# Graph network on one core: in the later two aggregations the source features become the stationary operand and the counts of three blocks the moving one

## What is computed

```python
h = relu(layernorm(x))                        # aggregation 0: symmetric norm, elementwise product
out = segment_sum(norm * (h[dst] + (h[dst] * h[src]) @ W1.T + b1), dst)
x = x + leaky(out)
h = relu(layernorm(x))
for Ws, Wn, b in ((Ws0, Wn0, b0), (Ws1, Wn1, b1)):        # aggregations 1 and 2 (GraphSAGE)
    mean = segment_sum(h[src], dst) / max(deg, 1)
    h = h @ Ws.T + mean @ Wn.T + b            # relu between the two
x = x + h
```

## Time and profile before

| | us |
|---|---|
| median of 3 runs | 3779.3 |
| lowest and highest of them | 3773.09, 3781.85 |
| the profiled execution's time | 3776.64 |
| its span, first to last instruction | 3774.9 |
| PE busy in the span | 3351.2 |
| POOL busy | 2654.8 |
| DVE busy | 2582.9 |
| ACT busy | 2222.0 |

### The profile page before, as it was taken

One profiled execution on the slowest core, in us unless ns is written; L12 is line 12 of the kernel. 1 busy time (PEld: TensorE's weight loads), 2 busy tenths in 40 slices (PEclk: granted clock), 3 DMA queues, 4 the chain that ended last, 5 costly groups with the idle time before them and its releaser, 6 DMA issues.

```text
span 3774.9 us, 73929 instructions
## 1 busy us (share of the span) xinstructions
PE 3351.2 (89%) x26412; PEld 2819.8 (75%) x26412; DVE 2582.9 (68%) x7629; ACT 2222.0 (59%) x4235; POOL 2654.8 (70%) x2533
## 2 busy tenths in 40 slices
PE   0069899999999999998999999999998999999998
PEld 0045566666666666666898898898998999999898
DVE  5789889988888888784566667567664554455444
ACT  1524566666666666664667767677665555455454
POOL 7617877777767777773776676676656777777775
PEclk9999999999999999999999999999999999999999
DMA  7363355555555555558575665665669666677665
GB/s 195 88 137 106 107 160 150 155 156 173 157 161 153 169 163 158 167 158 269 190 235 185 203 218 165 209 210 165 230 205 303 237 231 229 225 236 236 219 233 168
DMA packets 368294, 708.74 MB, mean 188 GB/s; under 512 B 66926, under 2 KB 284115, under 8 KB 345147
## 3 DMA queue, kind: packets, MB, share of 16 engines
q1 hardware_dynamic: 193794, 384.17, 29.6%
q0 software_dynamic: 116048, 284.86, 26.4%
q10 hardware_dynamic: 58080, 34.88, 3.1%
HBM read 530.06 MB, written 174.54 MB: 187 GB/s over the span
## 4 chain that ended last, share of the span: by engine, by line
PE 55%; POOL 22%; issue 8%; DVE 7%; DMA 4%; ACT 4%; ACTq 0%; DVEq 0%; POOLq 0%
PE ps L1686 38%; POOL ring_r L1454 15%; PE ps L1650 8%; PE ps L1591 5%; POOL arena L1454 4%; POOL arena L1429 3%; DVE arena L1978 3%; DVE arena L1983 2%; PE ps L1626 2%; DMA ring_r<-parts,arena 2%; ACT arena L1239 2%; ACT cast_r L1355 1%; DMA arena<-parts,arena 1%; PE ps L1604 1%; PE ps L1616 1%
## 5 line engine op out<-in xcount | busy, mean ns | idle before, releaser
L1454 POOL DMA_INDIRECT ring_r<-parts,arena x1322 | 1411.6, 1068 | 615.3 <-issue 395.1
L1686 PE MATMUL ps<-Xr,cast_r 128*128 128x256 f32 (+1 forms) x12544 | 1742.9, 292 | 14.5 <-DMA Xr<-parts 11.9
L1686 PEld LDWEIGHTS ps<-Xr,cast_r 128*128 128x128 f32 x12544 | 1626.6, 193 | 22.8 <-issue 9.3
L1239 ACT ACTIVATE arena<-ps 128x392 fp8e3<-128x392 f32 x2048 | 1006.9, 498 | 662.1 <-PE ps L1650 641.5
L1355 ACT ACTIVATE cast_r<-arena 128x896 fp32r<-128x896 fp8e3 x1024 | 956.0, 949 | 672.5 <-PE ps L1686 670.3
L1454 POOL DMA_INDIRECT arena<-parts,arena x984 | 1065.2, 1082 | 315.4 <-issue 294.8
L1650 PE MATMUL ps<-arena 128*128 128x196 bf16 (+1 forms) x5550 | 1141.2, 240 | 75.7 <-ACT arena L1239 41.2
L1686 PE MATMUL ps<-arena 128*128 128x388 bf16 x4900 | 1121.2, 328 | 32.3 <-DVEq L2057 29.9
L2161 DVE CAST cast_r<-arena 128x896 fp32r<-128x896 fp8e3 x768 | 500.8, 652 | 768.0 <-PE ps L1686 765.0
L1650 PEld LDWEIGHTS ps<-arena 128*128 128x128 bf16 x5550 | 520.7, 100 | 317.8 <-ACT arena L1239 82.7
L1978 DVE TENSOR_TENSOR arena<-arena 128x384 bf16<-128x384 bf16 (+4 forms) x1618 | 563.0, 380 | 157.6 <-PE ps L1650 149.5
(11 more groups left out here) (187 smaller groups left out, 1569.0 us busy)
## 6 DMA issues: line engine op xcount, KB each, us to landing
arena<-counts SPq DMA_DIRECT2D x110, 1568.0 KB
counts<-arena SPq DMA_DIRECT2D x64, 1568.0 KB
Xr<-parts SPq DMA_DIRECT2D x28, 896.0 KB, 12.4
ring_r<-parts,arena POOLq DMA_INDIRECT x1322
arena<-table SPq DMA_DIRECT2D x294, 64.0 KB
arena<-parts,arena POOLq DMA_INDIRECT x984
parts<-arena ACTq DMA_DIRECT2D x110, 128.0 KB
parts<-arena SPq DMA_DIRECT2D x86, 128.0 KB
```

Of the source, the lines that this page charges most:

```text
L1239: act.activation(stage[k][:, :, a - g * P:b - g * P], ps[:, unit_bank(q), 0:(b - a) * tiles].rearrange("p (n a) -> p a n", n=b - a), ACT.C ...
L1454: pool.indirect_dma_start(to, None, parts_of[nth], bass.IndirectOffsetOnAxis(ap=tail_idx[:, i, first + c:first + c + 1], axis=0)).then_inc ...
L1686: m = pe.matmul(bank(b, 0, w), counts_of, rows_of, start=e == 0, stop=e == tiles - 1, skip_group_check=True)
```

## The change

The dense products of stages 1 and 2 change sides. The stationary operand is one part (128 columns) of a source tile of `Xr`; the moving operand is that source tile's counts of three blocks side by side (384 columns). A bank then holds the sums of three blocks turned: features down the partitions, destinations along the columns. When a group of three blocks is done, ACT copies the 384 columns out (`sum_out`), and PE turns them back with three transposes (`turn_back`); `take` then reads a dense block's sum from PSUM without the reduction over parts. Dense blocks are 66 in stage 1 and 69 in stage 2, so 22 and 23 groups; the tails' visits become 617 and 554. 16 blocks (50 to 65) are built in stage 1 and three (66 to 68) in stage 2.

A piece is now 2 source tiles of three blocks (768 columns, 4 products) with 5 buffers, every other one cast by DVE. Counts are loaded by slabs of 14 source tiles of three blocks (672 KB, rows of 1792 bytes, 3 buffers). Visits are issued four at a time, every third piece, 16 times for a block; one ACT instruction evicts the two banks of four visits (784 columns). Blocks are built 57 pieces apart. The check of a built block reads a column of the result and no longer needs the 2 extra columns of `Xr`.

```diff
-STEPS = (50, 64, 64)
+STEPS = (50, 66, 69)
-ONES = (5, 3, 3)
+ONES = (4, 2, 2)
+LATE_HOTS = 2
+WIDTH = 3
+RUN = 2
+SLAB = 14
+SLABS = 3
-PIECES = 4
+PIECES = 5
-FIRST_DUE = 150
+FIRST_DUE = 40
+BUILD_FROM = 40
+BUILD_GAP = 57
+BUILD_GO = 3
+TILE_GAP = 6
...
-        by_vector = [g % 7 in (1, 3, 5) for g in range(len(stream))]
+        by_vector = [g % 2 == 1 for g in range(len(stream))]
...
+            for i, f in enumerate(goes):
+                add(hots_at, begin + BUILD_GO * i + 1, f)
+                add(visits_at, begin + BUILD_GO * i, f)
+                add(evicts_at, begin + BUILD_GO * i + PIECES, units_of[g][2 * i])
...
-            return cast_r[:, g % PIECES * HALF:(g % PIECES + 1) * HALF, :], stage[stage_of(nth, s)][:, a:a + HALF, :]
+            of = slabs[b % SLABS].rearrange("p b (a n) -> p b a n", n=P)[:, :, a:a + RUN, :]
+            return cast_r[:, g % PIECES].rearrange("p a b n -> p b a n"), of
...
+            def load_slab(b):
...
+                if b >= SLABS:
+                    last = (b - SLABS + 1) * runs_in - 1
+                    sp.wait_ge(s_castA, casts_to[0][last])
+                    sp.wait_ge(s_castV, casts_to[1][last])
...
+                sp.dma_start(slabs[b % SLABS], counts[g:g + WIDTH, :, a * P:(a + SLAB) * P].rearrange("b p c -> p b c")).then_inc(s_slab[b % SLABS], 16)
...
+            def evict_two(q):
...
+                act.wait_ge(s_visit, visits_to[q + 1])
...
+                    act.activation(built[:, :, a - g * P:a - g * P + 2 * n].rearrange("p a (k n) -> p k n a", k=2),
+                                   ps[:, LATE_BANKS[0]:LATE_BANKS[1] + 1, 0:n * tiles].rearrange("p k (n a) -> p k n a", n=n),
+                                   ACT.Copy, saturate=False).then_inc(s_evict, 2)
+
+            def sum_out(nth, s):
...
+                act.activation(turned_sum, bank((n - GROUPS) % 2, 0, WIDTH * P), ACT.Copy).then_inc(s_sum, 1)
...
+            def turn_back(nth, s):
+
+                n = groups_before[nth] + s - GROUPS
+                pe.wait_ge(s_sum, n + 1)
+                for k in range(WIDTH):
+                    t = pe.transpose(bank(n % 2, k * P, (k + 1) * P), turned_sum[:, k * P:(k + 1) * P], ident[:, :])
+                t.then_inc(s_turned, 1)
...
+            def piece(g):
...
+                for i in range(RUN):
+                    for k in range(2):
+                        m = pe.matmul(bank(n % 2, 0, WIDTH * P), Xr[:, a + i, k * P:(k + 1) * P], cast_r[:, g % PIECES, i, :, :].rearrange("p b n -> p (b n)"),
+                                      start=c == 0 and i == 0 and k == 0, stop=c == pieces_in - 1 and i == RUN - 1 and k == 1, skip_group_check=True)
+                m.then_inc(s_agg if c == pieces_in - 1 else s_piece, 1)
```

More of the change, by code:

```diff
@@ L30 @@
 PAIR = 2 * P
-ROWS = PAIR + 2
 EPS = 1e-5
@@ L191, in program @@
     tails_of = [tiles - n for n in STEPS]
+    groups_in = [0] + [n // WIDTH for n in STEPS[1:]]
+    assert all(n % WIDTH == 0 for n in STEPS[1:])
+    slabs_in, runs_in = tiles // SLAB, SLAB // RUN
+    pieces_in = tiles // RUN
     first_sub = [subs_of[STEPS[nth] - GROUPS][0] for nth in range(3)]
-    steps_before = [sum(STEPS[:nth]) for nth in range(4)]
+    groups_before = [GROUPS + sum(groups_in[:nth]) for nth in range(4)]
     tails_before = [sum(tails_of[:nth]) for nth in range(4)]
@@ L225, in program @@
[L225 to L235, removed]
+    steps = STEPS[0]
@@ new lines, in program @@
+    ends_at = {e + 1 + (e >= PAUSE - 1): i for e, i in enumerate(tail_order[0])}
+    assert len(ends_at) == tails_of[0] and max(ends_at) < steps
+    tail_at = [ends_at.get(s) for s in range(steps)]
+    places = 2 * steps + EMPTY
+    tile_at = [t for s in range(steps) for t in (None if tail_at[s] is None else GROUPS + tail_at[s], s)]
+    tile_at[-2:-2] = [None] * EMPTY
+    order = [[t for t in tile_at if t is not None]]
+    rank_at = [None if t is None else order[0].index(t) for t in tile_at]
@@ L319, in program @@
         stage = [view(k * C_COLS, tiles, P, dt=F8) for k in range(2)]
+        slabs = [view(at, WIDTH, SLAB * P, dt=F8) for at in (0, SLAB_COLS, 2 * SLAB_COLS + C_COLS)]
+        built = view(2 * SLAB_COLS, tiles, P, dt=F8)
+        assert 2 * SLAB_COLS <= C_COLS and len(slabs) == SLABS
         Xp = view(A_X, tiles, W0, dt=BF16)
@@ new lines, in program @@
+        land_before = {}
+        for g, ks in turn_at.items():
+            for k in ks:
+                nth = 1 if k + 2 < batches_to[1] else 2
+                if k + 2 < batches_to[1] or batches_to[1] <= k < n_batches - 2:
+                    land_before[next((nth, n) for n in sub_order[nth] if sub_due[nth][n] >= g + 8)] = k + 2
+        slabs_at = {}
+        for b in range(SLABS, len(stream) // runs_in):
+            add(slabs_at, (b - SLABS + 1) * runs_in - PIECES + 2, b)
+        ahead_at = {}
@@ new lines, in product @@
+            def product(s, e):
+                last = s == GROUPS - 1
+                a = (first_freed[e // HALF] if last else e // HALF) * HALF + e % HALF
+                if last and e == 0:
+                    w1_product(2 * s - 1)
+                if e == 0:
+                    pe.wait_ge(s_evict, evicts_of[s])
+                    if s == 0:
+                        pe.wait_ge(s_split0, halves)
+                        pe.wait_ge(s_tailrel, 2)
+                    else:
+                        pe.wait_ge(s_free, s)
+                m = pe.matmul(bank(2, 0, W0), stage[s % 2][:, a, :], Xp[:, a, 0:W0], start=e == 0, stop=e == tiles - 1, skip_group_check=True)
@@ new lines, in take_late @@
+            def take_late(n):
+                nth, r = n // tiles, n % tiles
+                t, e, m = order[nth][r], r % 2, tiles + r
+                if t < STEPS[nth]:
+                    s = next(s for s in range(groups_in[nth]) if group_at[nth][s] <= t < group_at[nth][s] + WIDTH)
+                    k, i = groups_before[nth] + s - GROUPS, t - group_at[nth][s]
+                    dve.wait_ge(s_turned, k + 1)
+                    of = bank(k % 2, i * P, (i + 1) * P)
+                    if STEPS[nth - 1] <= t:
+                        dve.tensor_scalar(agrees[:, t:t + 1], bank(k % 2, i * P, i * P + 1), 0.0, 0.0, ALU.mult, ALU.is_equal)
```

952 lines of the change are left out of this document (479 added, 473 removed).

## The result

The changed kernel takes 4411.7 us at the median of 4 runs (4410.05 to 4414.89), beside 3780.1 for the kernel before: 1.168 of it, with a 95% interval of 1.166 to 1.170. 3766 was forecast, with a range up to 3850.

The account below looks back on a forecast made before the run. Stage 1 was taken as bound by PE, stage 2 by POOL's gathers with PE close behind. From 3776.6 us, 6 less in stage 1 and 7 in stage 2 gave 3764; adjusted to the runs' median, 3766, range 3685 to 3850.

Parts of the forecast that it names:

- the eviction's price: Building turns: one ACT eviction of 784 columns taken at 0.85 us, between 0.83 and 0.996.
- Rival (c): Stages 1 and 2: building is tied up by DVE and ACT, so the kernel is slower, 3842 us; chance 0.18.
- Its threshold: 304 turns of four visits: 0.3 us of waiting counted in each; from 0.37 the kernel is slower than before.
- The product: PE, stages 1 and 2: a float32r product of 384 columns taken at 0.175 us, 1544 us for all 8820.
- rival (b): PE's products: columns alone count, 0.163 us each, giving 3679 us; chance 0.19.
- POOL no longer sets stage 2: Stage 2: POOL's gathers need 748 us against PE's sum of 886, so they no longer set the end.
- The cast on ACT: ACT: a cast of 768 columns taken at 0.81 us, scaled from 0.949 for 896.
- The slabs: Transfers of 672 KB land in 9.3 us or less, asked for 11 us ahead; waits of casts near nothing.
- rival (d): The 315 slab transfers come late behind SP's queue; one in three late by 0.7 us, 3840 us; chance 0.08.
- the waits at its start and of its three blocks: Stage 2: 12 us at the start, 4 for the first gathers, 5 for each built block.
- POOL's cover in stage 2: Stage 2: 99 us of cover used up by dearer products (43), building and turning back (25), less 13 of tails; 42 left.
- The odd outermost count of the cast: DVE's cast with outermost count 3: estimated 0.07 us above 0.65 by the port rule, left out of the sum.

Follow-up runs that it names:

- e13: Changed kernel with its eviction written in runs of 8 neighbouring bytes, one line changed: 3719.9 us beside 3769.1 for the kernel before, 0.987.
- e2: Changed kernel with the eviction cut into two instructions of one bank each, byte order kept: 4999.5 us beside 4580.7 for the kernel before.
- e9: Changed kernel unedited, run again on a slower chip: 5034.3 us beside 4574.4 for the kernel before, 1.099.
- e10: Changed kernel with the eviction in runs of 8 bytes, on a slower chip: 4404.3 us beside 4574.4 for the kernel before, 0.961.
- e3: Kernel before with only stage 1's evictions written in the change's order: 5121.0 us beside 4580.7 for the kernel before.
- e4: Single instructions on an otherwise idle core, no reference computed: 392 values evicted in 0.50 us in runs of four bytes, 1.91 as single bytes 128 apart.
- e14: e13 with casts written straight through and the eviction 3 slots behind the visits, not 5: 3688.2 us beside e13's 3719.9, 0.979 of the kernel before.

## Why the prediction was wrong, step by step

**The step that failed** is the eviction's price: "two of 392 are 2 x 0.498 = 0.996 from above ... I take 0.85". The row is right, but it is of another instruction. I took columns and types to be the price and did not ask in which order they are written; 128x98x4 against 128x8x98 stood in my own order rows. It measured 3.717, 4.4 times the term. ACT was busy for 833 us more in stages 1 and 2 than in e13 (1397 + 653 against 697 + 520), of which ACT's idle time hid some 140: the spans differ by 693. Four comparisons leave no other cause: the order alone makes the eviction dear in the changed kernel (e2, e9 and e10), in the kernel before (e3) and alone (e4). The Trainium skill (SBUF — State Buffer, section Door 1: The DMA port swizzle) would have warned: it says that accesses to SBUF which stay in one 16-byte line run at full rate and that each one that goes to a new line pays. The runs agree for bytes and bf16 128 bytes apart (1.91 us for 392 against 0.50); but runs of four bytes, each in a new line, paid nothing, and floats 64 bytes apart, each in a line of its own by that rule, cost 0.82, so the line alone does not give the price.

**Rival (c)** had the place right: building tied up by ACT. Its threshold, slower from 0.37 us of waits a turn, was passed by far, and no run tests it closely: in the changed kernel the waits in stage 1 were 419 / 256 = 1.64 us a turn. But it named DVE's cast as what would tip it, with 0.18 and 3842; the cast was 0.705, and DVE was idle. And it had no term for the clock, some 170 us in stage 1.

**What held.** The product: 0.175 forecast, 0.174 in the kernel and 0.1734 alone, so rival (b), 0.163, fell. POOL no longer sets stage 2: PE waited 1.2 us for gathered rows there in e13, where the kernel before had 54.8. The cast on ACT, 0.844 in stage 1 of e13 for 0.81. The slabs: casts waited 28 us on each of the two engines for transfers in stage 1, 17 of them in one wait, so rival (d) fell. Without the failed term, stage 1 is 1073 where 1085 stood, and stage 2 893 where 917 stood. The first is partly luck, two errors that nearly cancel: PE was busy for 1012 us where the sum had 982, 11 of these by the clock, and idle for 61 where it had 103 (23 of other waits and 80 of building). The second I had too dear by the waits at its start and of its three blocks, of which PE shows 10 us idle in all where I had 31. So the change with its one line mended is 1.3% faster, where the same sum with 0.174 for the product gave 3757. One slip changed nothing: POOL's cover in stage 2 was left at 42 us, and PE's sum of 886 leaves 38 of 924.

**The odd outermost count of the cast** was weighed in the prediction by the Trainium skill (Vector Engine (DVE) Microarchitecture Reference, section 5.1), as an estimate, at 0.07 us over 0.65, and left out of the sum; the kernel's mean of 0.705 agrees better with the estimate than with 0.65. The same section of the Trainium skill grants two ports only where the outermost count is even, or odd and the same in source and destination. The access patterns in the traces agree. The medians are 0.693 us with 3 outermost on both sides (the changed kernel), 0.560 with 2 outermost in the source and one run written (e4 and e14), 0.628 for one run of 896 (the kernel before), and 0.953 with one run read and 3 outermost written (e4). If the first three split over two ports into 512, 384 and 448 steps, and the last took all 768 on one port, all four lie within 0.01 us of one line, 0.16 us and 1.04 ns for each step (an estimate from these four rows). No run changed the count alone.

## What to carry over

An instruction's price belongs to its whole access pattern, not to its columns and types: before taking a row of the trace for a rewritten instruction, compare which index runs innermost on the side that is written. When a change trades many small steps for one large one, work out the turn of the loop with the new step at twice and four times its price, and see at which factor the engine that was idle becomes the bound. Here 0.85 and 1.5 casts of 0.81 stood in a turn of 2.5 us, and 1.5 times the price would have filled it.

## What the runs showed of the hardware

- Writing to SBUF on ACT: 392 values in jumps of 128 bytes took 1.91 us as bytes and as bf16, 0.82 as floats (64 bytes apart), 0.50 in runs of four bytes; the order in which PSUM is read made no difference (0.50). On DVE bytes took 1.90 singly and 0.57 in runs of four (e4).
- A float32r product costs the bf16 time and 0.011 to 0.012 us more at 256, 384 and 512 columns; at 128 and 192 columns it stays at 0.114 and 0.113 (e4).
- DVE's fp8 cast of 768 columns took 0.953 us with one run read and 3 blocks outermost in what is written (e4), 0.693 at the median with 3 outermost on both sides (the changed kernel), and 0.560 with 2 outermost in the source and one run written (e4, e14).
- PE's waits came twice: as idle time and as a lower granted clock behind it, 408 and some 170 us in stage 1 (the changed kernel beside e13).
